# A two-layer sequence block on one core: the same instructions of five engines in another order, and the PSUM banks dealt out anew

## The reference, cut to what matters

```python
# layer 0: cross attention, 16 heads of 16
q = relu(x @ Wq + bq); k = relu(ctx @ Wk + bk); v = relu(ctx @ Wv + bv)
a = softmax(where(row_mask, q_ @ k_.T / 4, 1e-9))       # per head
h = layernorm(merge(a @ v_) + x) * gamma + beta
# layer 1a: Mamba2 block, 8 heads of 64, state 128
z, xBC, dt = split(rms(h) @ in_proj_w)                  # 512, 768, 8 columns
dt = softplus(dt + dt_bias)
xs, B, C = split(silu(conv4(xBC) + conv_b))             # 4 taps, causal
s_t = exp(dt_t * A) * s_(t-1) + dt_t * xs_t B_t ;  y_t = s_t C_t
h = h + rms((y + D_skip * xs) * silu(z)) * gnorm_w @ out_proj_w
# layer 1b: cross attention, 8 heads of 32
out = h + softmax(layernorm(h) @ Wq1 @ (ctx @ Wk1).T / sqrt(32)) @ (ctx @ Wv1) @ Wo
```

## Time and profile before

| | before |
|---|---|
| median of 3 runs | 1318.08 us (1318.04 to 1318.75) |
| span of the profiled execution, first to last instruction | 1319.5 us |
| granted TensorE clock, whole span | 1.000 |
| PE busy | 1303.4 us, 99% |
| PE weight load busy | 1165.5 us, 88% |
| DVE busy | 1193.6 us, 90% |
| ACT busy | 1131.2 us, 86% |
| POOL busy | 947.7 us, 72% |
| data transfers (queue of SP) | 83.93 MB, 20.4% of 16 DMA engines |

### The profile page before, as it was taken

The page is one execution under the profiler, slowest core; times in us unless marked ns, Lnnn a source line. Parts: engine busy times, 40 slices in busy tenths (PEclk is TensorE's granted clock), DMA queues, the critical chain, the costliest instruction groups (busy, mean ns, idle before and its releaser), DMA issues.

```text
span 1319.5 us, 43916 instructions
## 1 busy us (share of the span) xinstructions
PE 1303.4 (99%) x15877; PEld 1165.5 (88%) x15877; DVE 1193.6 (90%) x3032; ACT 1131.2 (86%) x3407; POOL 947.7 (72%) x1214
## 2 busy tenths in 40 slices
PE   8999999999999999999999999999999999999998
PEld 7888888999888898888998888899888889898887
DVE  6999999999999999999999999999999999999882
ACT  6778888898888898888898888899888899888866
POOL 4777777777777777777677777687777677677674
PEclk9999999999999999999999999999999999999999
DMA  6121122212122212122211122211122222011210
GB/s 208 48 74 50 50 74 78 78 49 67 50 70 78 78 50 66 50 70 78 78 57 59 50 70 78 78 60 57 50 70 78 77 82 62 17 51 58 66 49 25
DMA packets 41285, 87.03 MB, mean 66 GB/s; under 512 B 5744, under 2 KB 10992, under 8 KB 41072
## 3 DMA queue, kind: packets, MB, share of 16 engines
q1 hardware_dynamic: 40560, 83.93, 20.4%
q10 hardware_dynamic: 512, 0.31, 0.1%
HBM read 75.53 MB, written 8.68 MB: 64 GB/s over the span
## 4 chain that ended last, share of the span: by engine, by line
PE 92%; DVE 4%; POOL 2%; issue 1%; DMA 1%; ACT 1%; DVEq 0%; ACTq 0%; POOLq 0%
PE bank L332 28%; PE bank L442 11%; PE bank L573 7%; PE bank L432 5%; PE bank L399 5%; PE bank L456 5%; PE bank L556 5%; PE bank L587 4%; PE bank L692 4%; PE bank L627 3%; PE bank L380 3%; PE bank L648 3%; PE bank L677 2%; PE bank L490 2%; PE bank L436 1%; PE bank L531 1%
## 5 line engine op out<-in xcount | busy, mean ns | idle before, releaser
L991 DVE SCALAR_TENSOR_TENSOR ACC<-bank,cw,ACC 128x250 f32<-128x250 f32 (+2 forms) x576 | 264.5, 462 | 6.4 <-ACT ACC L1561 3.7
L332 PE MATMUL bank<-xnT,wnl 128*128 128x256 f32 x640 | 198.6, 310 | 1.7 <-DVE XC L1004 1.4
L1648 ACT ACTIVATE PC<-bank,stc 128x128 f32<-128x128 f32 x512 | 182.8, 388 | 8.0 <-DVE stc L1103 5.2
L332 PE MATMUL bank<-xnL,wnh 128*128 128x256 f32 x640 | 178.7, 279 | 0.0
L332 PE MATMUL bank<-xnT,wnh 128*128 128x256 f32 x640 | 178.3, 279 | 0.0
L835 DVE TENSOR_REDUCE sta<-bank 128x4 f32<-128x512 f32 x256 | 163.6, 672 | 2.8 <-PE bank L399 2.8
L1015 DVE TENSOR_TENSOR_SCAN L<-DB,id 128x1024 f32<-128x1024 f32 x64 | 146.6, 2290 | 2.2 <-DMA DB<-dec_scratch 2.2
L1967 POOL TENSOR_TENSOR PC<-PC,stc 128x512 f32<-128x512 f32 x128 | 132.4, 1043 | 11.7 <-DVE stc L1110 11.5
L1463 ACT ACTIVATE PTA<-bank 128x512 f32<-128x512 f32 x256 | 133.5, 629 | 6.8 <-PE bank L436 3.9
L332 PEld LDWEIGHTS bank<-xnT,wnl 128*128 128x128 f32 x640 | 120.4, 188 | 21.4 <-issue 16.2
L1922 POOL TENSOR_TENSOR XH<-XH,dtt 128x512 f32<-128x512 f32 x64 | 81.0, 1265 | 56.6 <-ACT XH L1578 56.6
(11 more groups left out here) (210 smaller groups left out, 4757.7 us busy)
## 6 DMA issues: line engine op xcount, KB each, us to landing
DB<-dec_scratch SPq DMA_DIRECT2D x64, 512.0 KB, 4.0
cT<-in_cT SPq DMA_DIRECT2D x64, 256.0 KB, 2.7
xt<-in_xt SPq DMA_DIRECT2D x32, 256.0 KB, 3.7
out_x<-X SPq DMA_DIRECT2D x32, 256.0 KB, 4.0
xT<-in_xT SPq DMA_DIRECT2D x31, 256.0 KB, 4.1
QM<-qm_rows SPq DMA_DIRECT2D x31, 128.0 KB, 4.0
XC<-in_win SPq DMA_DIRECT2D x2, 644.0 KB, 6.8
PTC<-in_wout SPq DMA_DIRECT2D x2, 256.0 KB, 4.6
```

The costliest lines, as they stand in the source:

```text
L332: mm = e.matmul(t[:, c0:c0 + T], wt[:, k, m:m + 128], x[:, k, :], start=(n == 0), stop=(n == 5))
L991: e.scalar_tensor_tensor(out=w, in0=t[:, 0:T].rearrange("p (b t) -> p b t", b=NB)[:, :, 0:125 + k], scalar=cw[:, c, k:k + 1], in1=w, op0=A ...
L1648: op = e.activation(PC[n % 4][:, p, :], t[:, p * 128:(p + 1) * 128], ACT.Exp, bias=stc[g % 4][:, 4 * i + p:4 * i + p + 1], accum_out=stc[g ...
```

## The change

All five lists are written in another order, in the loop, the prologue and the epilogue; the table `USES` follows PE's. Calls and their counts are the same, `unread` and `warm` too. One wait is added, in `xs(0, 0)`. The edits of the loop, and of SP's list whole:

```diff
 USES: the rows follow PE's new order; steps with another bank:
-    sT: 4->1, 5->5, 0->3, 1->5, 2->0, 3->6     sA: 4->4, 5->5, 7->7
+    sT: 4->5, 5->1, 0->5, 1->6, 2->3, 3->0     sA: 4->5, 5->7, 7->4
@@ sync @@
-            load_x(1); load_c(1); load_t(0); load_m(1); load_x(2); load_m(2); load_c(2); load_c(3)
-            load_m(3); load_x(3); load_t(1); load_x(4); load_m(4); dec_out(0); dec_in(0, 0); load_t(2); dec_in(0, 1)
-            load_u(0); dec_out(1); load_c(4); dec_in(1, 0); dec_in(1, 1); load_u(1); load_t(3); load_x(5)
-            dec_out(2); load_c(5); dec_in(2, 0); load_x(6); dec_in(2, 1); load_m(5); load_u(2); load_t(4)
+            load_x(1); load_c(1); load_m(1); load_x(2); load_c(2); load_t(0); load_x(3); load_m(2); load_m(3)
+            load_t(1); dec_out(0); load_x(4); load_c(3); dec_in(0, 0); dec_in(0, 1); load_u(0); load_x(5); load_m(4)
+            dec_out(1); load_t(2); dec_in(1, 0); load_c(4); dec_in(1, 1); load_u(1); load_t(3); dec_out(2)
+            dec_in(2, 0); load_c(5); load_x(6); load_m(5); load_t(4); dec_in(2, 1); load_u(2)
             for g in range(NG - 9):
+                dec_out(g + 3)
+                load_m(g + 6)
                 load_c(g + 6)
-                dec_out(g + 3)
                 dec_in(g + 3, 0)
-                load_m(g + 6)
+                dec_in(g + 3, 1)
+                load_u(g + 3)
+                store(g)
                 load_x(g + 7)
-                load_u(g + 3)
-                dec_in(g + 3, 1)
                 load_t(g + 5)
-                store(g)
-            store(NG - 9); dec_out(NG - 6); load_c(NG - 3); dec_in(NG - 6, 0); load_m(NG - 3); load_m(NG - 2)
-            dec_in(NG - 6, 1); load_x(NG - 2); load_u(NG - 6); load_t(NG - 4); load_c(NG - 2); store(NG - 8)
-            dec_out(NG - 5); load_x(NG - 1); dec_in(NG - 5, 0); load_m(NG - 1); dec_in(NG - 5, 1); load_u(NG - 5)
-            dec_out(NG - 4); load_c(NG - 1); load_t(NG - 3); dec_in(NG - 4, 0); dec_in(NG - 4, 1); load_u(NG - 4)
-            load_u(NG - 3); load_t(NG - 2); store(NG - 7); dec_out(NG - 3); dec_in(NG - 3, 0); dec_in(NG - 3, 1)
-            dec_out(NG - 2); store(NG - 6); load_t(NG - 1); load_u(NG - 2); dec_in(NG - 2, 0); dec_in(NG - 2, 1)
-            store(NG - 5); dec_out(NG - 1); load_u(NG - 1); dec_in(NG - 1, 0); dec_in(NG - 1, 1); store(NG - 4)
+            load_x(NG - 2); dec_out(NG - 6); store(NG - 9); load_c(NG - 3); load_m(NG - 3); dec_in(NG - 6, 0)
+            dec_in(NG - 6, 1); load_u(NG - 6); dec_out(NG - 5); load_t(NG - 4); dec_in(NG - 5, 0); dec_in(NG - 5, 1)
+            load_c(NG - 2); load_m(NG - 2); load_x(NG - 1); load_u(NG - 5); load_t(NG - 3); dec_out(NG - 4)
+            load_c(NG - 1); store(NG - 8); dec_in(NG - 4, 0); load_m(NG - 1); dec_in(NG - 4, 1); load_u(NG - 4)
+            load_t(NG - 2); dec_out(NG - 3); dec_in(NG - 3, 0); dec_in(NG - 3, 1); store(NG - 7); store(NG - 6)
+            load_t(NG - 1); load_u(NG - 3); dec_out(NG - 2); store(NG - 5); dec_in(NG - 2, 0); load_u(NG - 2)
+            dec_in(NG - 2, 1); dec_out(NG - 1); dec_in(NG - 1, 0); store(NG - 4); dec_in(NG - 1, 1); load_u(NG - 1)
             store(NG - 3); store(NG - 2); store(NG - 1)
@@ vector, xs @@
                     ns = 2 * g + b
+                    if ns == 0:
+                        e.wait_ge(d_small, 16 * 4)
                     e.wait_ge(s_bg, ns + 1)
@@ tensor, loop: the moved steps @@
                 q(g + 7, 1)
-                k(g + 7, 0)
                 tC(g + 2, 2)
                 gm(g + 4, 0)
                 q1(g + 3, 0)
+                k(g + 7, 0)
                 sA(g + 6, 1)
...
                 nt(g + 5, 0)
-                gm(g + 4, 1)
                 sC(g + 3, 0)
                 oC(g + 2, 0)
                 oC(g + 2, 1)
+                gm(g + 4, 1)
                 cp(g + 5, 0)
...
                 v1(g + 3, 0)
+                wp(g + 2, 0)
                 cp(g + 5, 2)
-                wp(g + 2, 0)
                 tn(g + 6, 0)
...
                 cp(g + 5, 5)
+                tn(g + 6, 1)
                 av(g + 6, 0)
                 av(g + 6, 1)
                 av(g + 6, 2)
                 av(g + 6, 3)
-                tn(g + 6, 1)
                 tC(g + 3, 0)
@@ vector, loop: cut to what the prediction speaks of @@
                 tap(g + 5, 10)
+                tap(g + 5, 11)
                 hm(g + 4, 0)
-                tap(g + 5, 11)
...
                 scan(g + 5, 0)
                 mA(g + 7, 0)
                 kk1(g + 4, 1)
+                mA(g + 7, 1)
+                mA(g + 7, 2)
+                x2(g + 6, 0)
                 rc(g + 6, 1)
-                mA(g + 7, 1)
+                mA(g + 7, 3)
                 xo(g + 6, 1)
-                mA(g + 7, 2)
-                mA(g + 7, 3)
+                nm(g + 7, 0)
+                lg(g + 5, 0)
...
                 mC(g + 4, 0)
                 lg(g + 5, 1)
-                mC(g + 4, 1)
-                mC(g + 4, 2)
                 d0(g + 6, 0)
                 d0(g + 6, 1)
+                mC(g + 4, 1)
+                nm(g + 7, 1)
+                nw(g + 7, 0)
                 rC(g + 4, 0)
+                mC(g + 4, 2)
                 tap(g + 6, 0)
-                nm(g + 7, 1)
@@ scalar, loop @@
                 hx(g + 2, 0)
-                pC(g + 1, 1)
-                split_c(g + 6)
+                hx(g + 2, 1)
                 oa(g + 4, 1)
                 xhe(g + 3, 0)
-                hx(g + 2, 1)
-                n1(g + 4, 0)
+                split_c(g + 6)
                 he(g + 2, 0)
                 qe(g + 6, 0)
+                he(g + 2, 1)
                 qe(g + 6, 1)
-                he(g + 2, 1)
                 pC(g + 1, 2)
+                n1(g + 4, 0)
+                ke(g + 6, 0)
                 q1e(g + 2, 0)
+                nx(g + 4, 0)
                 n1(g + 4, 1)
-                ke(g + 6, 0)
                 split_x(g + 7)
-                nx(g + 4, 0)
+                ve(g + 6, 0)
                 nx(g + 4, 1)
-                ve(g + 6, 0)
                 q1e(g + 2, 1)
                 xhe(g + 3, 1)
...
+                zt(g + 4, 0)
+                th(g + 4, 0)
                 yh(g + 3, 1)
-                th(g + 4, 0)
                 qq(g + 3, 1)
                 th(g + 4, 1)
-                zt(g + 4, 0)
...
+                th(g + 4, 2)
                 da(g + 4, 0)
-                th(g + 4, 2)
...
+                nt_(g + 5, 1)
                 pC(g + 2, 0)
-                nt_(g + 5, 1)
@@ gpsimd, loop @@
+                qm(g + 6, 0)
                 ga(g + 3, 0)
+                dx(g + 3, 1)
+                qm(g + 6, 1)
                 xd(g + 3, 1)
                 s2_(g + 3, 0)
                 yl(g + 3, 0)
-                dx(g + 3, 1)
-                nC(g + 2, 0)
+                lo_x(g + 7)
                 ga(g + 3, 1)
                 r2(g + 3, 0)
+                nC(g + 2, 0)
                 yl(g + 3, 1)
                 s2_(g + 3, 1)
                 nC(g + 2, 1)
+                r2(g + 3, 1)
                 lo_u(g + 3)
-                qm(g + 6, 0)
-                r2(g + 3, 1)
-                qm(g + 6, 1)
                 hr(g + 3, 0)
-                lo_x(g + 7)
+                xr(g + 5, 0)
+                dx(g + 4, 0)
                 hr(g + 3, 1)
                 nC(g + 2, 2)
                 nC(g + 2, 3)
-                xr(g + 5, 0)
-                dx(g + 4, 0)
                 rs(g + 5, 0)
                 lo_c(g + 7)
                 xd(g + 4, 0)
@@ prologues, cut @@
-            w_hi(0)
-            mA(0, 0); mA(0, 1); mA(0, 2); mA(0, 3); nm(0, 0); nw(0, 0); mA(0, 4); mA(0, 5); mA(0, 6); mA(0, 7)
+            mA(0, 0); mA(0, 1); mA(0, 2); mA(0, 3); nm(0, 0); nw(0, 0); mA(0, 4); mA(0, 5); mA(0, 6); w_hi(0)
+            mA(0, 7); nm(0, 1); nw(0, 1); rc(0, 0); xo(0, 0); bs(0, 0); bg(0, 0); xs(0, 0); x2(0, 0); mA(1, 0)
...
-            qm(0, 0); qm(0, 1); lo_x(1); lo_c(1); lo_x(2); qm(1, 0); qm(1, 1); xr(0, 0); lo_c(2); rs(0, 0); xr(0, 1)
+            qm(0, 0); qm(0, 1); lo_x(1); lo_c(1); qm(1, 0); qm(1, 1); lo_x(2); xr(0, 0); lo_c(2); rs(0, 0); xr(0, 1)
@@ tensor, epilogue, from sC of group 31 on @@
-            oC(NG - 2, 0); oC(NG - 2, 1); unread("v1", 0, NG - 1, 12); wp(NG - 2, 0); tC(NG - 1, 0); v1(NG - 1, 0)
-            tC(NG - 1, 1); tC(NG - 1, 2); unread("tC", 3, NG - 1, 6); tC(NG - 1, 3); oC(NG - 1, 0); oC(NG - 1, 1)
+            unread("v1", 0, NG - 1, 12); oC(NG - 2, 0); oC(NG - 2, 1); v1(NG - 1, 0); wp(NG - 2, 0); tC(NG - 1, 0)
+            unread("tC", 3, NG - 1, 6); tC(NG - 1, 1); tC(NG - 1, 2); tC(NG - 1, 3); oC(NG - 1, 0); oC(NG - 1, 1)
             wp(NG - 1, 0)
```

613 lines of the change are left out of this document (301 added, 312 removed), and 16 rows, old and new, of the table USES.

## The result

The changed kernel takes 1415.26 us (median of 4 runs, 1410.85 to 1418.51) against 1318.17 (4 runs of the kernel before beside it): a ratio of 1.0728, 95% interval 1.0705 to 1.0752. The forecast was 1314.9, its range ended at 1324, and no rival reached this far. 97 us were to be explained.

The account below looks back on a forecast made before the run. PE bounds the kernel, idle almost only at the two ends. Loop -1.0, start 0, burst -1.7, end -0.5 sum to -3.2 us: from 1318.08 to 1314.9 us, range 1309.5 to 1324.

Parts of the forecast that it names:

- DVE's and POOL's other moves: Loop: moving x2 0, dx 1 and qm stays within both engines' idle time and costs nothing.
- The term of `av`: Loop: tap 11 ahead of hm 0 lets av 4 to 7 lose its 0.12 us wait; gain 2.8 us.
- The wait of `q1`: Loop: without k 0 between, q1 0 waits for qe 1 on ACT, 0.08 us an iteration; loss 1.8 us.
- `xT` arrives in time: Loop, SP's list: load_x comes later, slack falls from some 11 us to 0.2 to 0.6; priced at 0.
- rival (b): Loop: xT lands too late, PE waits at nt in each iteration; 1326.4 us, slower; chance 0.22.
- The burst term: End: a smaller burst of SP's transfers shortens PE's 2.23 us wait for instructions near 1240 us; -1.7 us.
- rival (a): End: the instruction fetch is late anyway, so no gain from the burst; 1316.6 us, no change; chance 0.22.
- The end: Rest of the end: filler ahead of oC and tC falls where PE waits anyway; -0.5 us, from -2 to +1.
- the start: Prologue: later parameters against fewer waits on DVE and filler in PE's gaps; 0, from -2 to +2 us.
- (c): Both ends: new lists save a third of PE's 12 us idle; about 1311 us, faster; chance 0.10.

Follow-up runs that it names:

- e5: Kernel before with an appended measurement of scans, two-operand VectorE steps and GpSimd passes, alone and side by side; scan and pass together: one pair each 3 us.
- e2: Changed kernel with GpSimd's loop call dx(g+3,1) moved back behind yl(g+3,0): 1402.83 us, ratio 1.0633.
- e10: Changed kernel with GpSimd's loop calls nC(g+2,2) ahead of xr(g+5,0) and rs(g+5,0) ahead of nC(g+2,3): 1396.1 us.
- e11: As e10, with GpSimd's qm 0, dx 1 and qm 1 also moved behind yl 0 in the loop: 1374.87 us.
- e8: Changed kernel with GpSimd's large passes cut to 4 columns from group 6 on, orders and waits kept: 1342.18 us, ratio 1.0171.
- e17: Kernel before with the head of GpSimd's new loop (qm 0, ga 0, dx 1, qm 1, then xd 1): 1321.66 us, ratio 1.001.
- e18: As e17, with nC 2 and nC 3 also moved behind dx(g+4,0), ahead of rs(g+5,0): 1347.8 us, ratio 1.021.
- e6: e2 plus a wait in GpSimd's loop, so ga(g+3,0) starts only behind the second scan of its group: 1410.0 us.
- e12: Kernel before with only VectorE's tap(g+5,11) moved ahead of hm(g+4,0) in the loop: 1316.67 us, ratio 0.9978.
- e16: e12 with SP's whole new list and the wait in xs(0,0): 1323.62 us, ratio 1.0024.
- e4: Changed kernel with SP's list put back to that of the kernel before: 1421.34 us, ratio 1.0768.
- e15: e12 with only the epilogue of SP's list new: 1323.64 us, ratio 1.0021.
- e3: Kernel before with only GpSimd's dx(g+3,1) moved directly behind ga(g+3,0) in the loop: 1319.01 us, ratio 0.9999.
- e13: e11 with PE's wp behind cp 2 and gm 1 ahead of sC as before, bank table to match: 1367.53 us, ratio 1.0349.
- e7: As e6, with another wait on GpSimd, for the first scan, ahead of rs(g+5,0): 1396.14 us.

## Why the prediction was wrong

**The step that failed** is one sentence: "DVE's and POOL's other moves (`x2` 0 two `mA` later, `dx` 1 earlier, `qm` earlier) are within their own idle time, DVE 10% and POOL 28%, and cost nothing while PE's banks have slack." It takes durations for constants and idle time for a reserve to be spent anywhere. Both are false here. In the kernel before, much of GpSimd's idle time lay where DVE scans (in one iteration it stands for 2.8 and 1.9 us around the scans at 251.87 and 263.34), and there both ran at full pace: scans at 2281 ns, `x2` at 480. The new list fills those places. In the loop it sets `ga` and `dx` beside the second scan (+1.06 us for DVE, +2 for POOL), `rs` beside the first (+2), `xd` beside `x2` (+0.7), and `nC` beside `hm` 1. e5 shows the exclusion, e2, e10 and e11 undo parts of it, e8 all of it together with the passes' length, e17 and e18 make some of it anew. In the loop DVE's busy time went from 36.8 to 39.2 us an iteration, nearly the whole of the old period of 39.5. The sentence also leaves out the move that proved dearest: `xr` and `dx` ahead of `nC` 2 and 3, so that these stand beside `hm` 1 and push `rs` into the first scan. e10, which undoes it, gives back 19 us.

`hm` needs a word, for it shows how this could have been seen. Two instructions of one column, `hm` 0 and 1, took 0.72 and 0.48 us before and take 0.15 and 0.99 now. In sum nothing has changed, but now the late one stands ahead of `kk1`, on which `sA` waits. The prediction looked at the 0.71 us of `hm` 0, called its reader not in haste, and did not ask why one column should take 0.71 us. The timeline of the kernel before answers it; DVE:

```profile
757.44 0.72 DVE L1081 SCALAR_TENSOR_TENSOR stb<-stb 128x1 f32<-128x1 f32 x1
```

and POOL, `lo_x`:

```profile
756.85 1.29 POOL L1842 TENSOR_TENSOR xL<-xT,xH 128x512 fp32r<-128x512 f32 x1
```

`lo_x` ends at 758.14, `hm` 0 at 758.16: it stood for 0.56 of its 0.72 us behind a GpSimd pass. `lo_c` gave the same hint, with 1903 ns on average in the kernel before where its shortest took 1284. Both were there to read before the prediction.

**The 2.8 us of period.** PE idles 37.5 us in 909 at 42.3 an iteration, 1.75 us each. The rest of the 2.8 I can place only in part. The granted clock is 0.99 over the loop: an iteration like 290.6 to 332.8 has 1.00 and takes 42.2 us, one like 389.3 to 432.3 has 0.96 and takes 43.0. In the latter the lower of the two levels, 1.2 instead of 2.4 GHz, was granted once, with PE at work in it, some 2.5 us behind a pause of 0.87 us for `nl`:

```profile
416.50:418.50 2.00, 2.00 (x11) 2.00 (x10) 1.82 (x4) 1.88 (x12) 2.00 (x2) 0.50 0.00 0
```

Seven of the 23 iterations have such a stretch and last about 1 us longer: 0.3 us on average. It did not occur in the loop of the kernel before, where PE never paused, but neither did it in e6, with pauses of 1.8 us an iteration and clock 1.00; so what brings it about stays open. The remaining 0.7 or so are presumably waits that overlap with a shown duration; that was not separated.

**What held.** The term of `av` was right in mechanism and size: forecast 2.8 us, e12 2.9, with 0.10 to 0.12 a period. The wait of `q1`, priced at 1.8 us of loss, is nearly absent: 0.1 us in all among PE's waits of the changed kernel. `xT` arrives in time, as the sum took it and against rival (b); e16 confirms it. Up to `k` of group 1 the changed kernel has lost 3.0 us in its profile (18.7 to 21.7), beyond the +2 allowed. SP's late parameters are not the whole of it: with SP's old list (e4) `k` still stands at 20.4, the kernels with the new prologue lie between 19.3 and 21.7, and e16 loses 0.5 there and nothing in time against e15.

**What else failed.** The burst term, -1.7: its wait was of one execution (e3, e5, e12 and e17 lack it with the burst as heavy as before), as rival (a) had it, and the new epilogue that should have gained it loses 6 us in e15 by a late store and a late `DB` load. That a packet of the queue "instruction" held PE up is shown by no run, so the 2.23 us say nothing on instruction fetch either. "DMA: Bandwidth & Descriptors" in the Trainium skill, cited in the prediction, left no gain for this term, and e15 shows none. The end, priced at -0.5, and the start at 0 cost 33 us together: the order of the ends makes about 25 of them on either loop, the rest stays with the new loop between old ends.

**The rivals.** (b) was slower in sign but through another mechanism, at 1326 by its price: it did not occur. (a) was right on the burst, (c) wrong in sign, and both were about terms too small to matter. The range's top came from 23 x (0.15 + 0.1); a bound for "moves cost nothing" had to ask what a collision of two engines costs, and the nearest row for that (`hm` 0, 0.56 us behind `lo_x`) gives 23 x 0.56 = 13 us for a single one an iteration.

**Open**: how the 2.8 us split into instructions that stand and results that are late by GpSimd's own order; the 0.73 us an iteration that e13 keeps; which parts of the five engines' end lists make the 25 us (SP's tail some 6 of them, if it costs there what it costs in e15). A mended loop with every end tuned to it was not tried.

## What to carry to other kernels

Before moving anything on GpSimd or VectorE, compare each form's mean with its shortest twin. A 128x1 operation shown with 0.7 or 2.2 us is not slow, it stands behind the other engine, and no list of waits will say so. The word "issue" in a chain is not yet a pause of PE either: look at PE's own starts (e12 has 4.10 us of it while PE works). Idle time of GpSimd beside scans and two-operand VectorE instructions is not spare: place GpSimd's passes beside reductions, taps and other work that reads PSUM, by order of the calls. A wait put in for it can move the loss (e6, 7 us worse than e2) or give some back (e7, 14 us better than e6). And a schedule's slack hides the first delays, so a single move that costs nothing (e3, e17) is no proof that the next one will cost nothing either (e18).

## What the runs showed of the hardware

- A scan of 128x1024 (2.27 us) and a GpSimd pass of 128x512 (1.04 us) alternate, one pair each 3.0 us (e5); each is shown as 3.0 to 3.1 us long.
- A one-column GpSimd operation can take 2219 ns instead of 203 (e5). A 128x256 VectorE instruction with two SBUF operands takes 1.18 us from start to start beside passes instead of 0.40; with one operand in PSUM nothing changes on either side.
- PE stands over 2 us with no releaser in the records in two of twenty profiles: 2.23 us at 1240.21 in the kernel before, and 6.69 at 1366.36 in e4. For the second the trace has a cause: the matmuls behind it read what a scan made, and that scan had waited 6.66 us for its load.

```profile
1369.33 2.29 DVE L1017 TENSOR_TENSOR_SCAN L<-DB,id 128x1024 f32<-128x1024 f32 x1 [6.66 <-DMA DB<-dec_scratch]
```

- With PE pausing 1.75 us an iteration in pieces of up to 1.3 us, the granted clock of the changed kernel fell to the lower level once in seven of 23 iterations (0.96 over such an iteration). With 1.8 us an iteration in pieces of at most 0.7 us (e6) it stayed at 1.00, as with no pause at all (kernel before, 900 us).
